# Masked attention over 8192 keys on one core: two of eight DMA-turned blocks go to TensorE, and the adjacency loads to ScalarE's queue

## What is computed

```python
h = relu(layernorm(x))
scores = h @ ks.T                                 # 8192 x 8192
scores = leaky_relu(scores, 0.2)
scores = where(adj > 0, scores, -9e15)
attn = softmax(scores, axis=1)
return x + attn @ ks
```

## Time and profile before

| | us |
|---|---|
| median of 3 runs | 1802.88 |
| lowest, highest | 1799.99, 1807.59 |
| the profiled execution, device time | 1804.0 |
| its span in the trace | 1802.2 |
| PE busy in the span | 1617.3 (90%) |
| ACT busy | 1606.0 (89%) |
| DVE busy | 1564.4 (87%) |
| POOL busy | 750.0 (42%) |
| DMA packets, share of the 16 DMA engines | 97.7% |
| mean granted TensorE clock | 0.994 |

### The profile page before, as it was taken

One profiled execution on the slowest core, in us unless ns is written; L12 is line 12 of the kernel. 1 busy time (PEld: TensorE's weight loads), 2 busy tenths in 40 slices (PEclk: granted clock), 3 DMA queues, 4 the chain that ended last, 5 costly groups with the idle time before them and its releaser, 6 DMA issues. The chain is left out here.

```text
span 1802.2 us, 37484 instructions
## 1 busy us (share of the span) xinstructions
PE 1617.3 (90%) x13442; PEld 1185.6 (66%) x13442; DVE 1564.4 (87%) x2592; ACT 1606.0 (89%) x2081; POOL 750.0 (42%) x713
## 2 busy tenths in 40 slices
PE   5799898898898898898898998988988988989988
PEld 3466666676666676666676666666766666666666
DVE  7888898898888888888888888988988888888885
ACT  7798898898898898898898988988988988989988
POOL 1344344443443443443443443444434434434433
PEclk9899999999999999999999999999999999999999
DMA  7699999999999999999999999999999999999996
GB/s 216 189 241 232 243 237 242 244 230 242 240 237 239 238 241 235 245 239 234 245 232 242 241 234 243 234 237 250 231 242 245 227 245 238 221 246 242 234 246 125
DMA packets 613686, 421.91 MB, mean 234 GB/s; under 512 B 547968, under 2 KB 580736, under 8 KB 580736
## 3 DMA queue, kind: packets, MB, share of 16 engines
q1 hardware_dynamic: 613504, 419.53, 97.7%
HBM read 281.02 MB, written 4.19 MB: 158 GB/s over the span
## 5 line engine op out<-in xcount | busy, mean ns | idle before, releaser
L322 POOL TENSOR_TENSOR halves<-scores,halves 128x512 f16<-128x512 f32 x512 | 596.5, 1165 | 995.0 <-ACT halves L485 995.0
L607 DVE CUSTOM_DVE_ANT_0 scores<-ps_scores,mask,minus_scale 128x1024 f32<-128x1024 f32 x512 | 654.8, 1279 | 3.3 <-PE ps_scores L370 2.7
L468 ACT ACTIVATE scores<-scores,neg_max 128x1024 f32<-128x1024 f32 x512 | 582.3, 1137 | 0.0
L461 ACT ACTIVATE scores<-scores 128x1024 f32<-128x1024 f32 x512 | 537.6, 1050 | 9.8 <-DVE pair_min L607 9.7
L368 PE MATMUL ps_scores<-keysT_hi,hT_hi 128*128 128x512 f16 x1024 | 390.2, 381 | 166.3 <-DVE hT_lo L536 154.1
L616 DVE TENSOR_TENSOR probsT_lo<-ps_T,probsT_hi 128x512 f16<-128x512 f32 x512 | 351.8, 687 | 192.2 <-ACT probsT_hi L476 192.0
L476 ACT ACTIVATE probsT_hi<-ps_T 128x512 f16<-128x512 f32 x512 | 305.6, 597 | 167.5 <-PE ps_T L379 161.9
L394 PE MATMUL ps_out<-keys,probsT_hi 128*128 128x258 f16 x2048 | 399.6, 274 | 6.3 <-issue 4.5
L370 PE MATMUL ps_scores<-keysT_hi,hT_lo 128*128 128x512 f16 x1024 | 390.4, 381 | 0.0
L589 DVE TENSOR_SCALAR mask<-adj_in 128x2048 bf16<-128x2048 int32 x256 | 390.1, 1524 | 0.1
L369 PE MATMUL ps_scores<-keysT_lo,hT_hi 128*128 128x512 f16 x1024 | 390.0, 381 | 0.0
(11 more groups left out here) (52 smaller groups left out, 749.1 us busy)
## 6 DMA issues: line engine op xcount, KB each, us to landing
adj_in<-in_adj_dram SPq DMA_DIRECT2D x256, 1024.0 KB, 5.6
turned<-halves SPq DMA_TRANSPOSE x512, 6.0
x_in<-in_x_dram SPq DMA_DIRECT2D x64, 64.0 KB, 5.3
keys_in<-in_L_gnn_ks_dram SPq DMA_DIRECT2D x8, 512.0 KB, 7.3
x_res<-in_x_dram SPq DMA_DIRECT2D x64, 64.0 KB, 4.9
out_dram<-out_tile SPq DMA_DIRECT2D x64, 64.0 KB, 5.3
```

The lines of the kernel that those rows point to most:

```text
L322: nc.gpsimd.tensor_tensor(half[:, BLOCK:2 * BLOCK], probs(t, b), half[:, 0:BLOCK], ALU.subtract) \
L461: nc.scalar.activation(s, s, ACT.Prelu, alpha=1.0 / SLOPE).then_inc(leaky_ready, 1)
L468: nc.scalar.activation(s, s, ACT.Exp, bias=neg_max[:, t % 2:t % 2 + 1], scale=-SLOPE) \
L607: nc.vector.tensor_tensor_reduce(out=score_pair(q, p), in0=ps_scores[:, slots, :].rearrange("p s k -> p (s k)"), in1=mask[:, (p // 2) % 2, ...
```

## The change

Three things change, and one small one.

1. `BY_DMA` loses blocks 7 and 15. They join `BY_PE`: ten blocks of a tile are turned by TensorE, six by DMA.
2. The adjacency loads are issued from ACT's instruction stream instead of SP's. The first two stand at its very start, the others in steps 2, 6, 10 and 14, ahead of the exponential of that step, each with the same wait for `mask_ready`. On SP they stood in steps 1, 5, 9 and 13.
3. `lift` is removed: `neg_max` is `plain_max` plus a constant. The chain of `minimum` has three instructions instead of four.
4. The tuples and helpers for a variant in which DVE makes the high half, which was never taken, are deleted.

```diff
-    BY_DMA = tuple(b for b in range(BLOCKS) if b % 2 == 1)
+    BY_DMA = tuple(b for b in range(BLOCKS) if b % 2 == 1 and b % 8 != 7)
     BY_PE = tuple(b for b in range(BLOCKS) if b not in BY_DMA)
...
-    LIFT = 14 * 0.6931471805599453
-    LIFT_BELOW = 2.0 ** 22
+    LIFT = 7.99
...
         def _(sp):
-            def load_adj(q, k): ...
-            load_adj(0, 0)
-            load_adj(0, 1)
...
                 for j in range(BLOCKS):
-                    if j % 4 == 1:
-                        q, k = divmod((i + 1) * LOADS + j // 4 + 2, LOADS)
-                        if q < TILES:
-                            load_adj(q, k)
...
         def _(act):
+            def load_adj(q, k):
+                if q > 0 or k >= 2:
+                    act.wait_ge(mask_ready, q * LOADS + k - 1)
+                act.dma_start(adj_in[:, k % 2, :], adj[rows(q), k * LOAD:(k + 1) * LOAD]) \
+                    .then_inc(adj_loaded[k % 2], 16)
...
+            load_adj(0, 0)
+            load_adj(0, 1)
             for b in range(BLOCKS):
                 copy_keysT(b)
...
+                    if j % 4 == 2:
+                        q, k = divmod((i + 1) * LOADS + j // 4 + 2, LOADS)
+                        if q < TILES:
+                            load_adj(q, k)
                     if j % 2 == 0:
                         made = behind(i, j, EXP_LAG, range(0, BLOCKS, 2), this, prev)
...
                 dve.wait_ge(plain_max_ready, q + 1)
-                nc.vector.tensor_scalar(lift[:, :], plain_max[:, :], plain_max[:, 0:1], LIFT_BELOW ** 2,
-                                        ALU.mult, ALU.is_lt) \
-                    .then_inc(lift_ready, 1)
-                dve.wait_ge(lift_ready, q + 1)
                 if q > 1:
                     dve.wait_ge(probs_ready, (q - 1) * PAIRS)
-                nc.vector.scalar_tensor_tensor(out=neg_max[:, q % 2:q % 2 + 1], in0=lift[:, :], scalar=LIFT,
-                                               in1=plain_max[:, :], op0=ALU.mult, op1=ALU.add) \
+                nc.vector.tensor_scalar(neg_max[:, q % 2:q % 2 + 1], plain_max[:, :], LIFT, None, ALU.add) \
                     .then_inc(neg_max_ready, 1)
```

More of the change, by code:

```diff
@@ L38, in gat_kernel @@
     HI_LAG = 2
-    HI_DVE_LAG = 3
     LO_LAG = 3
@@ L42, in gat_kernel @@
     ADD_LAG = 10
-    BY_DMA = tuple(b for b in range(BLOCKS) if b % 2 == 1)
+    BY_DMA = tuple(b for b in range(BLOCKS) if b % 2 == 1 and b % 8 != 7)
     BY_PE = tuple(b for b in range(BLOCKS) if b not in BY_DMA)
-    HI_ON_DVE = tuple(b for b in BY_DMA if False)
-    HI_ON_ACT = tuple(b for b in BY_DMA if b not in HI_ON_DVE)
     EPS = 1e-5
@@ L109, in gat_kernel @@
         plain_max = sbuf("plain_max", [P, 1], fp32)
-        lift = sbuf("lift", [P, 1], fp32)
         neg_max = sbuf("neg_max", [P, 2], fp32)
@@ L152, in gat_kernel @@
         plain_max_ready = sem("plain_max_ready")
-        lift_ready = sem("lift_ready")
         neg_max_ready = sem("neg_max_ready")
@@ L161, in gat_kernel @@
         half_hi_ready = sem("half_hi_ready")
-        half_hi_dve_ready = sem("half_hi_dve_ready")
         half_lo_ready = sem("half_lo_ready")
@@ L190, in nth_pe @@
             return t * len(BY_PE) + sum(c < b for c in BY_PE)
[L192 to L196, removed]
         def nth_dma(t, b):
@@ L244, in store @@
                 sp.dma_start(out[rows(t), :], out_tile[:, :]).then_inc(stored, 16)
[L246 to L250, removed]
             def turn(t, b):
@@ L316, in split_half_lo @@
                 n = nth_dma(t, b)
[L317 to L320, removed]
+                pool.wait_ge(half_hi_ready, n + 1)
                 half = halves[:, n % R_SLOTS, :]
@@ L508, in step @@
                         split_keys_hi(j // 2)
-                    split = behind(i, j, HI_LAG, HI_ON_ACT, this, prev)
+                    split = behind(i, j, HI_LAG, BY_DMA, this, prev)
                     if split:
@@ L617, in split_probs_lo @@
                                         ALU.subtract).then_inc(T_lo_ready, 1)
[L619 to L625, removed]
             def minimum(q):
@@ L689, in step @@
                         split_probs_lo(*split)
-                    split = behind(i, j, HI_DVE_LAG, HI_ON_DVE, this, prev)
-                    if split:
-                        split_half_hi(*split)
                     if ahead:
```

## The result

The changed kernel takes **1883.61 us** (1883.33 to 1884.76), and the kernel before, run beside it, 1804.49. The ratio is 1.0442 with a 95% interval of 1.0417 to 1.0466: 4.4% slower. The forecast was 1865, the range 1836 to 1903.

What follows compares the result with a forecast made beforehand. TensorE was taken to bound each tile: 24.90 us without a gap, then a 2.40 us stall. The terms 54 - 15.5 + 18.5 + 7 - 2 = +62 gave 1865 us, range 1836 to 1903.

Steps and rivals of the forecast that it cites:

- What bounds the kernel: Steady tile: 24.90 us of TensorE without a gap, then a 2.40 us stall; DMA and DVE full but late for nobody.
- Blocks on TensorE, +54: Blocks 7 and 15 turned by TensorE cost in full: 0.87 us a tile in 62 tiles, +54 us.
- `lift`, -15.5: Chain ending each tile: removing lift gains 0.25 us in each of 62 tiles, -15.5 us.
- The loads on ACT, +18.5: Adjacency loads issued from ACT cost 0.3 us in each of 62 tiles, +18.5 us; bounds 0 and 1.3 us a tile.
- The walk: New tile's end timed from its first score: TensorE and the mask-load-exponential chain meet within 0.02 us at step 14's probsT_hi.
- The 0.3: Microseconds a tile taken for load delays on ACT, between 0 (issue hidden) and 1.3 (load waits for a turning DMA's issue).
- rival B: Loads on ACT wait for turning DMAs that SP is issuing, 1.3 us a tile: 1885 to 1930 us, chance 0.2.
- The start, +7: First adjacency loads now run beside the key chunks, so the last chunk comes 7 us later if all share one rate.
- The end, -2: Block 15 comes through TensorE, so the last product's wait for a turned block shrinks: -2 us, bounds 0 and -3.
- the row that shows the price: After the one steady stall of 2.77 us, granted clock was 0.68 for 3.5 us; after 2.40 it was 1.00.
- A: ACT pays nothing for the loads and the start is nearly free: 1839 to 1846 us, chance 0.22.
- C: Faster: the DMA queue at 97.7% sets the tile, so fewer turned blocks shorten it: 1785 us, chance 0.04.

Runs made afterwards that it cites:

- the filled kernels: Eight unneeded matmuls in TensorE's wait for hT_lo, added to the kernel before with only the loads moved: 1812.05 us; with only the blocks moved: 1856.08 us.
- the early splits: Split of h (hT) moved from the end of step 15 to step 14, ahead of the last mask: kernel before 1654.77 us, changed kernel 1716.84 us.
- before, padded: Kernel before with three unneeded matmuls, 0.65 us of TensorE, added in step 3: 1881.07 us.
- after, stall filled: Changed kernel with eight unneeded matmuls in TensorE's wait for hT_lo at the tile's end: 1845.31 us, and 1845.3 us when run again.

## Why the prediction was right and where it wasn't

The direction was right, and the time lies in the range, but 1883.6 is at the far edge of the forecast's own 1847 to 1885, and it is made of other terms than the sum. Two errors of opposite sign, the loads put 18.5 too high and the clock's falls left out at 35 to 38, cancelled in part and left the 18.6 us by which the forecast is off. That it lies inside 1847 to 1885 is in part luck.

- **What bounds the kernel: right.** TensorE without a gap, and one stall a tile. Each full-clock tile, in the kernel and in its parts, is the sum of the two.
- **Blocks on TensorE, +54: right.** 0.87 us a tile (28.17 - 27.30; 0.93 in some tiles), 0.88 in the mean where nothing stalls (25.86 - 24.98), 52 us by the filled kernels. The Trainium skill's 275 ns for a transpose ("TensorE: Matmul & The Clock Gate", Part 4) would have made an estimated 136 us. The measured 52 to 53 for 8 in each of 62 tiles are 0.11 us each in a full stream.
- **`lift`, -15.5: right per tile, wrong in time.** The tile shrank by 0.24 to 0.25. Alone it was worth some 5 us of 15, since the shorter tile brought falls.
- **The loads on ACT, +18.5: mis-sized.** It measured nothing per tile in the changed kernel. The walk without the 0.3 gave 27.30 + 0.87 - 0.25 = 27.92, and the tile is 27.92 or 27.93. The walk's mask end of 22.42 was 22.38, and its `probsT_hi` at 23.83 was 23.85. The 0.3 was added for issues that block each other, and they don't (rival B, below).
- **The start, +7: a little too high,** 5.1. So the keys lost less than the full share that was assumed; why wasn't looked for. **The end, -2:** the last wait is 1.3 us shorter.
- **The missing term: the clock, +35 to 38.** The prediction had the row that shows the price. It read it as one that belongs to a *longer* stall, used it only in rival B, and let the steady tile run at full clock since its stall would get shorter. This is the step that failed. The stall did get shorter, 2.15 against 2.40, and falls came in 22 tiles of 60. With the loads at 0 and the falls at 38 the sum reads 54 - 15.5 + 5 - 1 + 38 = 80, that is 1804 + 80 = 1884.

**Rivals.** *A* (1839 to 1846) was right in its mechanism: the stall is its 2.15, the full-clock tile 27.92, and without falls the changed kernel takes 1845.3. *B* is refuted by the issues themselves. Two cases, of ACT's queue and what goes on beside it:

```profile
93.68 1.23 SPq L238 DMA_TRANSPOSE turned<-halves  x1
```

```profile
94.36 1.05 ACT L439 ACTIVATE scores<-scores 128x1024 f32<-128x1024 f32 x1
94.78 0.33 ACTq L418 DMA_DIRECT2D adj_in<-in_adj_dram  x1
```

```profile
1398.06 3.40 SPq L238 DMA_TRANSPOSE turned<-halves  x1
```

```profile
1400.14 0.33 ACTq L418 DMA_DIRECT2D adj_in<-in_adj_dram  x1
```

The first load is issued during ACT's own `leaky` and during the last 0.13 us of SP's turning issue, the second wholly inside a turning issue of 3.40 us. Both take 0.33. Of the 256 loads, 186 overlap an issue on SP, 5 of them lie whole inside a turning one, and behind the start of the program the longest took 0.37. Nor are they held back before they begin: the loads of steps 6, 10 and 14 are issued 0.03 us after the mask that they wait for has ended, whatever SP is at. The Trainium skill ("Perfetto Trace Analysis", "DMA Instruction — HWDGE") has a lock wait inside the profiled issue where two engines share the block. In the rows of the 5 loads no such wait shows, and the tile of 27.92 leaves no room for one. *C* (1785, the DMA queue sets the tile) is refuted by the early splits: at 1.12 DMA share, two turned blocks less still cost their transposes.

## To carry to other kernels

Where TensorE stalls once a period, read the granted clock of the stretch behind each stall over many periods, not of one tile: a period 0.1 us longer brought 44 us of falls here, and one 0.24 us shorter brought 13. A wait that can't be removed can be filled with matmuls that compute nothing, but first ask whether the work that ends it has to stand where it does: moving two instructions ahead of one that they don't depend on was worth 150 us, more than all the parts of the change together.

## What the runs showed of the hardware

The table gives, for each kernel, the full-clock distance between two row minima, TensorE's stall, how many of 60 steady intervals were lengthened by a fall of the granted clock to 0.50, and the mean interval. All are worked out from the traces, intervals by the starts of `row_min`.

| kernel | full-clock tile, us | stall, us | tiles with a fall, of 60 | mean tile, us |
|---|---|---|---|---|
| `lift` removed | 27.06 | 2.15 | 8 | 27.29 |
| before | 27.30 | 2.40 | 1 | 27.34 |
| loads on ACT | 27.40 | 2.50 | 26 | 28.09 |
| after, loads on SP | 27.91 | 2.14 | 21 | 28.50 |
| after | 27.92 | 2.15 | 22 | 28.55 |
| before, padded | 27.95 | 2.40 | 23 | 28.60 |
| blocks only | 28.17 or 28.23 | 2.40 or 2.46 | 31 | 29.06 |
| after, stall filled | 27.93 | 0.44 | 0 | 27.95 |

With the same stall of 2.15 there are 8 falls or 22, and with 2.40 (2.40 or 2.46 in the blocks alone) there are 1, 23 or 31. So the stall's length doesn't say how often the clock falls, while with the stall filled it never does in a steady tile. What goes with it is the tile's length: at 27.30 the falls are all but absent.

The falls also keep distances of their own. In the changed kernel they begin 85.3 or 58.0 us apart, in the padded one and in the one with the loads on SP the same two, in the one with the blocks only nearly always 58.0, in the one with the loads on ACT 27.3 or 58.0 by turns, and in the one without `lift` mostly 191.1, whatever the exact length of the tiles between them. That looks like something in the chip that runs on its own time, and a stall that brings a fall only where it meets it in a certain position.

The traces can test this, since their stalls lie in many positions at one tile length and one stall length. In each of these kernels all starts of falls behind the first 60 us fit one regular beat, the same in all of them, to 0.001 us, so the next beat can be told for every stall, with or without a fall. The 60 steady stalls of each kernel, by the distance from the stall's end to the fall or to the next beat:

| kernel | with a fall: start of the fall behind the stall's end, us | without one: next beat behind the stall's end, us |
|---|---|---|
| after | 22, 0.48 to 1.32 | 38, from 1.38 |
| after, loads on SP | 21, 0.78 to 1.34 | 39, from 1.39 |
| before, padded | 23, 0.74 to 1.29 | 37, from 1.38 |
| blocks only | 31, 0.46 to 1.37 | 29, from 1.40 |
| before | 1, 1.23 | 59, from 1.46 |

The two groups never overlap, at equal tile and stall. In the kernel before, 52 of the 59 stalls lie 1.46 to 1.72 us ahead of the next beat, just on the harmless side: a tile of 27.30 comes back to the same position each time, while the tiles of 27.9 to 28.2 drift through all of them. The other two kernels fit in part: in the one with the loads on ACT (stall 2.50) 14 falls start 1.13 to 1.36 behind the stall's end, and 12 already 0.39 to 0.77 ahead of it; without `lift` all 8 start between 0.28 ahead and 0.09 behind. So the position decides, and by it the tile's length. What in the chip keeps the beat, no run shows.

The Trainium skill ("TensorE: Matmul & The Clock Gate", "HAM oscillation — how this bites in real kernels") tells of a kernel whose clock falls anew behind each of its waits, and of the cure, to keep TensorE busy. The trace agrees on the cure, 38 us here. That falls can skip two stalls out of three, all of 2.15 us, or nearly all stalls of 2.40, by where these lie, is what these runs add.
